# Local attention: rotation partners swapped by DMA, residual kept shifted, a new order of the slot

## The reference, cut to what matters

```python
def shift_tokens(t):                      # second half of the channels comes one token late
    a, s = jnp.split(t, 2, -1)
    s = jnp.pad(s, ((0, 0), (1, 0), (0, 0)))[:, :-1]
    return jnp.concatenate([a, s], -1)
def rotate_half(x):
    x1, x2 = jnp.split(x, 2, -1)
    return jnp.concatenate([-x2, x1], -1)
def attn_layer(x, Wqkv, qs, ksc, Wo):     # 16 heads of 64
    q, k, v = heads(x @ Wqkv)
    q = l2norm(q) * qs; k = l2norm(k) * ksc
    q = q * cos * scale + rotate_half(q) * sin * scale
    k = k * cos / scale + rotate_half(k) * sin / scale
    return merge(local_attention(q, k, v)) @ Wo     # windows of 32, own and previous
for i in range(6):
    x = attn_layer(shift_tokens(x), ...) + x
    x = ffn_layer(shift_tokens(x), ...) + x         # layer norm, gelu gate, 341 wide
```

## Time and profile before

| | |
|---|---|
| median of 3 runs | 2607.53 us (2607.38 to 2608.51) |
| profiled execution | 2603.33 us, span 2601.5 us |
| granted TensorE clock, mean | 0.976 |
| TensorE busy | 2272.6 us, 87% |
| VectorE | 1972.9 us, 76% |
| ScalarE | 1820.0 us, 70% |
| GpSimd | 1082.0 us, 42% |
| DMA moved | 29.74 MB |

### The profile page before, as it was taken

One profiled execution on the slowest core, in us unless ns is written; L12 is line 12 of the kernel. 1 busy time (PEld: TensorE's weight loads), 2 busy tenths in 40 slices (PEclk: granted clock), 3 DMA queues, 4 the chain that ended last, 5 costly groups with the idle time before them and its releaser, 6 DMA issues. The chain is left out here.

```text
span 2601.5 us, 60924 instructions
## 1 busy us (share of the span) xinstructions
PE 2272.6 (87%) x24172; PEld 1056.4 (41%) x24172; DVE 1972.9 (76%) x2595; ACT 1820.0 (70%) x2593; POOL 1082.0 (42%) x461
## 2 busy tenths in 40 slices
PE   7788999989999899989999899998999787767778
PEld 2344444444444444444444444444444332222345
DVE  5678877787778877787777787788877568999442
ACT  4678777777777777777777777777777566545533
POOL 0344444444444444444444444444444204556030
PEclk8899999999999999999999999999999989999989
DMA  0100000000000000000000000000000010000001
GB/s 21 54 2 2 2 23 13 11 2 2 15 22 11 1 2 14 22 11 2 2 15 19 13 2 2 14 14 18 2 2 2 1 37 1 0 0 0 18 24 41
DMA packets 16036, 29.74 MB, mean 11 GB/s; under 512 B 3616, under 2 KB 6064, under 8 KB 15664
## 3 DMA queue, kind: packets, MB, share of 16 engines
q1 hardware_dynamic: 15760, 25.78, 3.1%
HBM read 24.73 MB, written 1.05 MB: 10 GB/s over the span
## 5 line engine op out<-in xcount | busy, mean ns | idle before, releaser
L708 POOL TENSOR_TENSOR f_rot<-f_raw,f_tabc 128x1024 f32<-128x1024 f32 x192 | 452.5, 2357 | 636.7 <-DVE f_qk L756 293.5
L712 POOL TENSOR_TENSOR f_rot<-f_rot,f_shuf 128x1024 f32<-128x1024 f32 x192 | 453.2, 2360 | 501.5 <-DVE f_shuf L749 501.5
L605 ACT ACTIVATE f_raw<-f_ps 128x1024 f32<-128x1024 f32 x192 | 196.7, 1025 | 234.7 <-PE f_ps L429 234.6
L756 DVE SCALAR_TENSOR_TENSOR f_qk<-f_rn,f_rot 128x1024 f32<-128x1024 f32 x192 | 234.2, 1220 | 72.5 <-POOL f_rot L712 72.5
L775 DVE TENSOR_REDUCE f_sum<-f_ps 128x8 f32<-128x512 f32 x192 | 131.9, 687 | 199.4 <-ACT f_ps L664 199.4
L434 PE MATMUL f_ps<-f_sq,f_same 128*128 128x512 f32 x384 | 206.9, 620 | 71.2 <-ACT f_sq L608 71.2
L746 DVE STREAM_SHUFFLE f_shuf<-f_raw 128x1024 f32<-128x1024 f32 x192 | 255.4, 1330 | 0.0
L428 PE MATMUL f_ps<-f_xs,f_wq 128*128 128x512 f32 x384 | 214.6, 641 | 35.6 <-DVE f_xs L727 35.2
L749 DVE TENSOR_TENSOR f_shuf<-f_shuf,f_tabs 128x1024 f32<-128x1024 f32 x192 | 236.8, 1233 | 7.6
L614 ACT ACTIVATE f_rn<-f_ps 128x1024 f32<-128x1024 f32 x192 | 197.6, 1029 | 41.7 <-PE f_ps L435 34.1
L616 ACT ACTIVATE f_rn<-f_rn,k_lift 128x1024 f32<-128x1024 f32 x192 | 220.8, 1150 | 6.3
(11 more groups left out here) (267 smaller groups left out, 3938.2 us busy)
## 6 DMA issues: line engine op xcount, KB each, us to landing
e_w<-in_e_w SPq DMA_DIRECT2D x16, 256.0 KB, 2.8
f_wq<-in_f_wq SPq DMA_DIRECT2D x12, 256.0 KB, 2.7
f_wk<-in_f_wk SPq DMA_DIRECT2D x12, 256.0 KB, 3.3
f_wv<-in_f_wv SPq DMA_DIRECT2D x12, 256.0 KB, 3.5
f_wo<-in_f_wo SPq DMA_DIRECT2D x6, 512.0 KB, 3.2
f_w<-in_f_w SPq DMA_DIRECT2D x6, 341.0 KB, 2.9
s_dx<-in_k_pick SPq DMA_DIRECT2D x1, 1536.0 KB, 8.8
f_w<-in_f_w SPq DMA_DIRECT2D x6, 192.0 KB, 3.2
```

Of the source, the lines that this page charges most:

```text
L708: pool.tensor_tensor(view(rot, 0, [S, 4], [1, S]), view(raw, 0, [S, 4], [1, S]), view(tab_c, 0, [S, 2], [0, 2], [1, S]), ALU.mult).then_in ...
L712: pool.tensor_tensor(rot[:, :], rot[:, :], shuf[:, :], ALU.add).then_inc(sem["rot"], 1)
L756: dve.scalar_tensor_tensor(out=view(qk[j % 2], 0, [KOFF, 2], [1, UNIT]), in0=view(rn, 0, [UNIT, 2], [1, UNIT]), scalar=1e12, in1=view(rot, ...
```

## The change

The partners are laid side by side (`dim_order`: even and odd partitions). SP copies the odd rows of `raw` to the even rows of `shuf` and the other way, with two DMAs for each head pair, as soon as `raw` is written and the sum of the pair before has read `shuf`. The shuffle on VectorE goes; `rotate` waits for both DMAs (a count of 32).

`y` becomes 257 columns for each sequence. The upper 64 partitions hold a token one column late, with a zero in front; so `shifted(u)` is the shifted unit without a copy and `tokens(u, g)` the plain one, for 64 partitions at a time. The matmuls read `y` directly; `shift_in`, `xs` and `xs2` go. Residual updates become two instructions. Ahead of the last norm the residual is copied to `flat`.

The order of the slot changes on TensorE and ScalarE. Variance and the last hidden block move; the inverse deviation is written to PSUM; tables are made once a layer; the loop has four units in its body and 5 passes, where it had two and 11.

```diff
+        def swap(sp, n):
+            need(sp, sem["raw"], n + 1)
+            need(sp, sem["rot"], n)
+            for g in range(2):
+                sp.dma_start(half_of(shuf, g), half_of(raw, 1 - g)).then_inc(sem["shuf"], 16)
...
+        def half_of(buf, g):
+            a = buf[g:g + 1, 0:1]
+            return bass.AP(a.tensor, a.offset, [[2 * a.ap[0][0], 64], [1, 2 * UNIT]])
...
+        shifted = lambda u: view(y, 2 * u * YB, [YB, 2], [1, S])
+        tokens = lambda u, g: view(y, 2 * u * YB + g, [YB, 2], [1, S], p0=64 * g, rows=64)
...
# TensorE, slot
                 if run:
                     scores(i, j)
-                if had2:
-                    mix(u2, b2)
-                if before and j == 2:
-                    wo_part(k, 6, 8)
                 if before and j == 6:
                     gate_mm(k, 1)
                     gate_mm(k, 2)
+                if had2 and j == 6:
+                    mix(u2, b2)
                 if has:
-                    if j == 7:
+                    if j >= 6:
                         values(...)
                     project(...)
-                    if j != 7:
+                    if j < 6:
                         values(...)
+                if had2 and j != 6:
+                    mix(u2, b2)
+                if before and j < 3:
+                    wo_part(k, 3 * j, min(3 * j + 3, NP))
                 if before and j == 3:
                     mean(...)
+                if before and j == 4:
+                    variance(k)
                 if before and j == 6:
                     hid_mm(k, 1)
                 if before and j == 7:
-                    hid_mm(k, 2)
+                    w2_mm(k)
                 if had1:
                     turn(u1, b1)
                 if has:
                     norms(u, a)
-                if before and j == 4:
-                    variance(k, run)
                 if before and j == 5:
                     gate_mm(k, 0)
                     hid_mm(k, 0)
-                if before and j == 7:
-                    w2_mm(k)
+                if before and j == 6:
+                    hid_mm(k, 2)
...
# ScalarE, slot: the exponential first, then raw_copy, out_copy, value_copy; out_copy first in slot 6 only
-                if had2:
-                    out_copy(u2, b2)
-                if has:
-                    raw_copy(u, a)
                 if run:
                     act.activation(..., ACT.Exp, scale=8.0).then_inc(sem["exp"], 1)
+                if had2 and j == 6:
+                    out_copy(u2, b2)
+                if has:
+                    raw_copy(u, a)
+                if had2 and j != 6:
+                    out_copy(u2, b2)
                 if has:
                     value_copy(u, a)
+                if before and j == 4:
+                    act.activation(sq2[:, :], bank(3), ACT.Ln, bias=con.eps)...
+                    act.activation(bank(3), sq2[:, :], ACT.Exp, scale=-0.5)...
...
# VectorE
-                dve.stream_shuffle(shuf[:, :], raw[:, :], [(p + 16) % 32 for p in range(32)])...
+                need(dve, sem["shuf"], (i * 8 + j + 1) * 32)
...
-                    dve.tensor_tensor(ycol, ycol, bank(3), ALU.add).then_inc(sem["y1"], 1)
-                    shift_in(xs2, k % NU, sem["xs2"])
+                    for g in range(2):
+                        ins = dve.tensor_tensor(tokens(mk, g), tokens(mk, g), pair_of(ps, 3 * CH, 64 * g, 64), ALU.add)
...
-                    dve.tensor_tensor(xn[:, :], cen[:, :], sq2[:, :], ALU.mult).then_inc(sem["scaled"], 1)
+                    dve.tensor_tensor(xn[:, :], cen[:, :], bank(3), ALU.mult).then_inc(sem["scaled"], 1)
```

More of the change, by code:

```diff
@@ L368, in local_attention @@
         n_const = 16 * len(consts)
[L370 to L378, removed]
+        NL = NU * NP
@@ new lines, in layer @@
+        def layer(sp, r, first, more):
+            for n in range(NL):
+                swap(sp, r * NL + n)
+                if not first and n == 6:
+                    need(sp, sem["wo_mm"], r * NU)
+                    load_out(sp, r)
+                if not first and n == 11:
+                    need(sp, sem["h_mm"], r * NU * 3)
+                    need(sp, sem["w2_mm"], r * NU)
+                    load_ffn(sp, r)
+                for k in range(2):
+                    if more and n == NL - 5 + 4 * k:
+                        need(sp, sem["a_mm"], r * NL + n + 1)
+                        need(sp, sem["v_mm"], r * NL + n + 1)
+                        load_in(sp, r + 1, k)
@@ L495, in wo_part, with mean, variance @@
                     mm.then_inc(sem["wo_mm"], 1)
[L497 to L501, removed]
+            def mean(i, m):
+                need(pe, sem["y1"], i + 1)
+                pe.matmul(pair_of(ps, 3 * CH), con.ones[:, :], shifted(m), start=True, stop=True).then_inc(sem["mean"], 1)
+            def variance(i):
                 need(pe, sem["sq2"], i + 1)
[L503 to L505 removed]
+                pe.matmul(bank(3), con.ones[:, :], sq2[:, :], start=True, stop=True).then_inc(sem["var"], 1)
             def gate_mm(i, f):
@@ L528, in w2_mm, with slot @@
                 mm.then_inc(sem["w2_mm"], 1)
-            def slot(i, j, run, more, before):
+            def slot(i, m, j, run, more, before):
                 k = i - 1
@@ L741, in rotate @@
             def rotate(i, j):
[L743 to L748, removed]
+                need(dve, sem["shuf"], (i * 8 + j + 1) * 32)
+                need(dve, sem["tab"], i // NU + 1)
                 dve.tensor_tensor(view(shuf, 0, [S, 4], [1, S]), view(shuf, 0, [S, 4], [1, S]),
@@ L847, in _ @@
             n1.vector_centre(dve, n1_banks, x)
-            n1.vector_scale(dve, y)
+            for c in range(NCH):
+                dve.wait_ge(n1.cen, n1.n + c + 1)
+                dve.wait_ge(n1.rs, n1.n + c + 1)
+                for g in range(2):
+                    ins = dve.tensor_tensor(tokens(c, g), pair_of(n1.c, c * CH, 64 * g, 64),
+                                            pair_of(n1.q, c * CH, 64 * g, 64), ALU.mult)
+                ins.then_inc(n1.out, 1)
             dve.wait_ge(n1.out, n1.n + NCH)
```

156 lines of the change are left out of this document (81 added, 75 removed).

## The result

The changed kernel takes 2520.12 us, median of 4 runs (2518.26 to 2520.7), beside 2608.02 us for the kernel before (4 runs, 2607.38 to 2610.49): a ratio of 0.966, 95% interval 0.9643 to 0.9677. The forecast was 2519.

What follows compares the result with a forecast made beforehand. TensorE sets the pace, losing 6.83 us a unit to ScalarE's order and VectorE's load. Saving 3.5 a unit gives 80 us over 23 units, plus 10 for loop edges, less 2 once-only: 88 saved, 2519 us, range 2465 to 2600.

Steps and rivals of the forecast that it cites:

- The slots: Slot lengths of one unit: 9.7 each for 0 and 1, 9.2, 8.5, 8.7, 10.9, and 21.6 for 6 and 7; sum 78.3.
- TensorE's own work: Slot 2: its length was taken as 9.2 us, set by the work of TensorE itself.
- The new wait: TensorE's transposes wait for ScalarE's out-copy, moved behind the square, as both use one bank; to be TensorE's largest named wait.
- out-copy chain: From the scores' end through the out-copy 4.9 us, then transposes, norm sums and next scores 3.28; taken as 8.5.
- The swap: Pair of DMAs on SP: 3.9 us from the end of the raw copy to the rotation, in a loop of 8.3.
- upper end: Swap by the pair of DMAs: 5.4 us if two landings come in a row.
- The third rival: The pair takes 5.4 us, the swap's loop of 9.95 sets the pace: unit 84.6, total 2664 us; chance 0.15.
- point of decision: The swap decides from about 4.9 us for the pair: loop 9.45, unit 82, no change.
- The second rival: ScalarE's out-copy, square and exponential half a us later in slots 2 to 7: unit 81.3, total 2588 us; chance 0.15.
- The first: Rival: pair lands in about 2.7, TensorE idle only 1 us a unit: 76.0 a unit, total 2466 us; chance 0.10.
- Half residual updates: VectorE: a 64-partition half priced like a whole, 0.68 us, so each residual update costs 0.7 more.
- loop edges: Ends of loop passes on TensorE: 1.7 us each; 5 passes instead of 11 save 10 us.

Runs made afterwards that it cites:

- three kernels with a part taken out: Changed kernel with the shuffle back on VectorE, 2523.49 us; with unshifted residual and shifted copies, 2517.33 us; with the old slot order, 2563.61 us.
- C: The new order on TensorE and ScalarE; the changed kernel with the old slot order instead measured 2563.61 us.
- A: The swap by DMA in place of the shuffle; alone on the kernel before 2570.69 us, changed kernel without it 2523.49 us.
- B: The shifted residual without copies; on the kernel before, with PSUM scaling and four-unit loop, 2547.51 us; changed kernel without it 2517.33 us.
- filled kernel: Changed kernel without slot 2's out-copy wait for the whole output projection, values ahead of projection in slots 0 to 2, behind in 6: 2471.2 us.
- serial kernel: Changed kernel with the second half of each swap issued only when the first has landed: 2593.2 us, ratio 0.9944.
- C alone: Kernel before with the new order, scaling from PSUM and the loop of four units; shuffle and shifted copies on VectorE: 2532.93 us.

## Why the prediction was right

*What bounds the kernel.* TensorE sets the pace, and what it loses, it loses to the order of the slot: shown by the three kernels with a part taken out. C was not taken apart, so that it is ScalarE's order more than TensorE's is argued. The prediction's view of A and B, that their worth is VectorE early again, holds where nothing else has made it early (36 and 58 us alone, the 58 with scaling and loop in it). It did not see that the three parts relieve the same waits.

*The slots.* The sum was forecast at 78.3 and is 78.46, partly by errors that cancel, so that the time came out within 2 us is in part luck. Slots 6 and 7 came to 21.59 without the edge (21.6), with the norm sums' wait in slot 6 at 1.04 (0.9). Slots 3 to 5 came out 8.43, 8.42 and 10.21 against 8.5, 8.7 and 10.9. Slots 0 and 1 are 0.2 longer than 9.7. In slot 1 that is the projection's wait on a logarithm that reads the same banks, which the prediction left out and which is gone there in the filled kernel (9.63); in slot 0 of the unit shown, behind a loop edge, no wait is named for it, but in a unit without an edge ahead slot 0 (717.65 to 727.52, 9.87) has the same wait of 0.20. Slot 2 is 10.04, not 9.2: "TensorE's own work" missed that the out-copy waits there for the output projection. Without that wait, in the filled kernel, the slot takes 9.19.

*The new wait* of the transposes on the out-copy is TensorE's largest named one, as predicted, but it stands in slots 2 and 5 only, not in 3 and 4. There TensorE is busy 8.15 of 8.43: its own work was 8.15, and the out-copy chain just fits.

*The swap* was sized too large: 2.98 us from raw copy to rotation, not 3.9, because one landing takes 2.3, not the 2.7 and 3.3 of the earlier trace rows, and the second follows some 0.6 us after the first. Little came of it, since either is hidden. Windows of 1 us of the changed kernel, over the swap shown above:

```profile
770.00:771.00 1.00, 0.41 (x4) 0.44 (x5) 0.00 (x0) 1.00 (x3) 1.00 (x1) 1.00 0.96 389
771.00:772.00 1.00, 1.00 (x6) 0.52 (x4) 0.15 (x1) 1.00 (x3) 0.31 (x1) 1.00 0.33 135
```

The bytes of both halves move in one stretch, at 389 GB/s in its first us; at that rate their 512 KB take 1.35 us. So it is the rest of a landing that the two share: made to follow each other they end in 4.53 us, not 2.98. The Trainium skill's "DMA: Bandwidth & Descriptors", "Rules for kernel authors", says that two transfers to disjoint halves of the partitions serialize, since they share the same engines, and advises one transfer instead. The trace agrees as far as the bytes go; two whole landings in a row, as the prediction read it for its upper end, did not come. Whether one transfer would be as quick as the pair was not tried.

*The third rival*, the swap as the pace, was right as a mechanism: the loop that it works out is the one in the timeline of the serial kernel. Its price was too small, in part since it counted no change of clock. Its point of decision, 4.9 us from the first issue, is close to where the measured lines cross (4.6 to 4.8 from the end of the raw copy).

*The second rival*, the order gives it back, is excluded: C alone saves 73, more than the scaling and the loop in it account for. *The first*, better than forecast, has its place in the filled kernel: 2471, where it had 2466 for TensorE idle 1 us a unit; but it takes two edits that the change does not make, and TensorE is idle for 2.3 us a unit there, so the nearness of the two times says little.

*The small terms.* Half residual updates cost a whole one, as taken, and loop edges are 1.5 each (four in 1500 us), near the 1.7 taken. The hand-over to the raw copy, priced at 0.04, takes 0.18 with the swap. The scaling alone is worth 15 us, more than the nothing on TensorE's path that the prediction gave it: in that kernel slot 5 takes 9.62 instead of 10.01 and slot 6 11.54 instead of 11.88, where the projection waits 0.85 us for the gelu and no longer 1.21 for the shifted copy. Its 2.40 us were also put down to two inputs in SBUF alone. Of the 24 scalings before, 23 overlap GpSimd's sum and take 2.4 us, as in slot 5 of the earlier trace rows; the last, with GpSimd idle, takes 0.69:

```profile
797.87 2.36 POOL L712 TENSOR_TENSOR f_rot<-f_rot,f_shuf 128x1024 f32<-128x1024 f32 x1 [2.75 <-DVE f_shuf L749]
798.38 2.40 DVE L827 TENSOR_TENSOR f_xn<-f_cen,f_sq 128x512 f32<-128x512 f32 x1 [0.65 <-ACT f_sq L679]
```

With one input in PSUM and the rest as before, all 24 take 686 to 690 ns, 23 of them beside the same sum. So it was two inputs in SBUF while GpSimd ran.

## What to carry to other kernels

Where several engines are tied in one slot, ask of each edit which wait of the bounding engine it ends: edits that end the same wait are paid once. A part that is worth nothing now can be worth 1% after the next wait goes, so measure it again before it is thrown out. A DMA in place of an engine's operation is hidden up to a point given by the loop of waits that it closes; work out that loop, and leave it room, for beyond it the clock can add to the loss. Then compare the hand-overs of the two traces, since the new waits can cost something where nobody looked.

## What the runs showed of the hardware

A pair of SBUF-to-SBUF DMAs of 256 KB each, 64 rows of 4 KB, lands within 2.98 us of the end of what it reads, hand-overs included; weight loads of the same size from HBM take 2.9 and 3.4 each in the same run.

After TensorE had been idle for 1.94 us in a busy stretch, the granted clock was 0.50 for about 3.4 us; after 1.14 us in the changed kernel it stayed at 1.00. But the length of the wait alone does not decide. Two slots 5 of the serial kernel, both with 1.87 us of it ahead of the transposes and the same instructions before:

```profile
629.29:640.24 10.95, 8.81 (x120) 4.30 (x119) 6.91 (x9) 9.18 (x15) 4.71 (x2) 1.00 0.13 53
...
1116.34:1128.97 12.63, 10.49 (x120) 5.15 (x119) 7.06 (x9) 9.28 (x15) 6.00 (x3) 0.86 0.23 87
```

In the first the clock stays at 1.00, in the second it falls. At the loop edges of the filled kernel it fell to 0.50 after 1.71 us (at 477.17) and stayed at 1.00 after 1.70 (at 785.28).

A copy of 128 x 9 elements on VectorE, 166 ns in the kernel before, takes 1741 ns after the change (1.50 here), and ends with the product on GpSimd beside it, 831.71 + 2.36 = 834.07:

```profile
831.71 2.36 POOL L749 TENSOR_TENSOR f_rot<-f_raw,f_tabc 128x1024 f32<-128x1024 f32 x1 [1.85 <-ACT f_raw L646]
...
832.60 1.50 DVE L847 TENSOR_SCALAR f_fcol<-f_cols 128x9 f32 x1
```

That is the rule of the Trainium skill's "SBUF — State Buffer", "Who interferes with whom": such a copy can want the ports that VectorE shares with GpSimd, and then waits until the other's instruction is done. The trace agrees. Here it is hidden.
